# The linear phase of a transformer kernel: its first steps rearranged, the sums of q squares moved beside those of u, and an output projection that waits part by part

## The reference, cut to what matters

```python
q = l2norm(silu(x @ Wq)); k = l2norm(silu(x @ Wk)); v = silu(x @ Wv)
g = sigmoid(x @ Wf - dt_bias); beta = sigmoid(x @ Wb); A = exp(-exp(A_log))
for t in tokens:                      # state: 64x64 for each sequence and head
    o_t = (q_t @ state) * g_t
    state = A * state + beta_t * outer(k_t, v_t)
o = o * rsqrt(mean(o*o) + eps) * norm_w          # over the 64 of a head
out = x + (o * sigmoid(x @ Wg + bg)) @ Wo
```

## Time and profile before

| | us |
|---|---|
| median of 3 runs | 904.65 (904.13 to 906.27) |
| the profiled execution | 908.08 |
| its span, first to last instruction | 906.0 |
| mean granted clock of TensorE | 0.974 |

### The profile page before, as it was taken

The page is one execution under the profiler, slowest core; times in us unless marked ns, Lnnn a source line. Parts: engine busy times, 40 slices in busy tenths (PEclk is TensorE's granted clock), DMA queues, the critical chain, the costliest instruction groups (busy, mean ns, idle before and its releaser), DMA issues.

```text
span 906.0 us, 31429 instructions
## 1 busy us (share of the span) xinstructions
PE 824.8 (91%) x13280; PEld 711.7 (79%) x13280; DVE 554.9 (61%) x1296; ACT 569.4 (63%) x1202; POOL 584.4 (65%) x514
## 2 busy tenths in 40 slices
PE   4858998999797799999999999999999999997877
PEld 3647997899695687888788788888888888885776
DVE  3976566567684356557467467467467467566473
ACT  4746554665565666767767767767767766754544
POOL 4983211320455788977977977977977977986322
PEclk9988999999997899999999999999999999997999
DMA  5001000100100000000000000000000000000011
GB/s 190 26 12 36 25 13 1 31 18 2 25 1 1 1 3 3 4 3 3 3 3 3 4 3 3 4 3 3 4 2 3 3 3 3 3 3 2 13 31 51
DMA packets 19417, 12.38 MB, mean 14 GB/s; under 512 B 7760, under 2 KB 18768, under 8 KB 19024
## 3 DMA queue, kind: packets, MB, share of 16 engines
q1 hardware_dynamic: 19280, 10.39, 4.0%
HBM read 8.29 MB, written 2.10 MB: 11 GB/s over the span
## 4 chain that ended last, share of the span: by engine, by line
PE 50%; DVE 9%; POOL 4%; issue 3%; ACT 2%; DVEq 0%; POOLq 0%; ACTq 0%
PE la_ps L1465 7%; PE la_ps L1467 6%; PE la_ps L1466 6%; DVE la_u_lo L1773 4%; PE la_o_ps L1528 4%; PE la_o_ps L1544 4%; PE la_s_ps L1558 4%; PE la_ps L1575 3%; PE la_ps L1509 3%; DVE la_u L1767 3%; PE la_ps L1609 2%; PE la_ps L1496 2%; PE la_ps L1610 2%; PE la_ps L1611 2%; PE la_ps L1598 1%
## 5 line engine op out<-in xcount | busy, mean ns | idle before, releaser
L2109 POOL TENSOR_TENSOR la_coef<-la_ssk,lt_mhalf 128x32 f32<-128x32 f32 x16 | 87.1, 5442 | 71.2 <-DVE la_ssk L1784 71.2
L1465 PE MATMUL la_ps<-la_x_hi,w_hi 128*128 128x256 f32 x384 | 116.7, 304 | 2.0 <-ACT la_v L1924 1.0
L1467 PE MATMUL la_ps<-la_x_hi,w_lo 128*128 128x256 f32 x384 | 107.6, 280 | 0.1
L1466 PE MATMUL la_ps<-la_x_lo,w_hi 128*128 128x256 f32 x384 | 107.5, 280 | 0.0
L2141 POOL TENSOR_TENSOR la_scale<-la_scale,lt_mhalf 128x32 f32<-128x32 f32 x16 | 99.9, 6241 | 6.7 <-DVE la_scale L1760 6.4
L1807 DVE TENSOR_TENSOR lt_state<-la_s_ps,la_faded 128x512 f32<-128x512 f32 x62 | 42.6, 687 | 70.6 <-PE la_o_ps L1544 57.5
L1465 PEld LDWEIGHTS la_ps<-la_x_hi,w_hi 128*128 128x128 f32 x384 | 72.4, 189 | 14.5 <-issue 6.2
L713 ACT ACTIVATE at_probs<-at_s_ps,at_ntop 128x512 f32<-128x512 f32 (+2 forms) x80 | 49.0, 623 | 46.5 <-DVE at_ntop L655 46.4
L598 PE MATMUL at_o_ps<-V,at_probsT 128*128 128x128 f32 x544 | 74.6, 277 | 3.2 <-DVE at_probsT L507 2.0
L531 POOL CAST at_q_hi<-qk_hi 128x128 fp32r<-128x128 f32 x32 | 9.4, 294 | 104.9 <-PE at_s_ps L572 102.4
L598 PEld LDWEIGHTS at_o_ps<-V,at_probsT 128*128 128x128 f32 x544 | 69.1, 192 | 6.5 <-ACT at_probsT L729 2.3
(11 more groups left out here) (216 smaller groups left out, 2501.3 us busy)
## 6 DMA issues: line engine op xcount, KB each, us to landing
at_w_raw<-in_w SPq DMA_DIRECT2D x20, 128.0 KB, 2.2
X<-in_x SPq DMA_DIRECT2D x8, 256.0 KB, 2.9
out<-X SPq DMA_DIRECT2D x8, 256.0 KB, 2.3
qkv_cos<-in_cos SPq DMA_DIRECT2D x1, 1024.0 KB, 5.0
qkv_sin<-in_sin SPq DMA_DIRECT2D x1, 1024.0 KB, 7.2
lt_w_out<-in_w_out SPq DMA_DIRECT2D x4, 128.0 KB, 2.7
const<-in_const SPq DMA_DIRECT2D x1, 320.5 KB, 3.3
qkv_w<-in_w_qkv SPq DMA_DIRECT2D x1, 320.0 KB, 3.9
```

Source lines behind the costliest of these rows:

```text
L1465: eng.matmul(out, l_hi, r_hi, start=True, stop=False)
L1466: eng.matmul(out, l_hi, r_lo, start=False, stop=False)
L1467: return eng.matmul(out, l_lo, r_hi, start=False, stop=True)
L2109: eng.tensor_tensor(coef[:, :], ssk[:, :], mhalf[:, :], ALU.pow).then_inc(s["coef_step"], 1)
```

## The change

Four things change. `sq` moves in the ring and on PE to right behind `su`, and gets a buffer of its own, `sq_q`, which ACT fills with one instruction behind the last silu of q, a step earlier. `project_out` waits for the low part of u in four parts. In steps -2 to 0 x of tile 1 is turned ahead of `k0` of step -1 (job `x1`), and the copies of it on ACT and `low_x(1)` on POOL move forward with it. The tables' clearing and selectors move from the linear block into the end of the ffn block, `tables.vector` moves the other way, and the first moments and normalized tiles move one and two slots ahead. ACT's list in the linear block begins with a silu of one column.

```diff
@@ ffn_phase, gpsimd slot
+                if next_norm is not None and g.off == GROUPS - 2:
+                    next_norm.first_gpsimd(eng)
                 if tables is not None and g.off == GROUPS - 1:
                     tables.gpsimd_strict(eng)
-                if next_norm is not None and g.off == GROUPS:
-                    next_norm.first_gpsimd(eng)
+                    tables.gpsimd_clear(eng)
+                    tables.gpsimd_selectors(eng)
@@ ffn_phase, vector slot
-                if tables is not None and g.off == GROUPS:
-                    tables.vector(eng)
-                if next_norm is not None and g.off == GROUPS:
-                    next_norm.first_vector(eng)
+                if next_norm is not None and g.off == GROUPS - 1:
+                    next_norm.first_normalized(eng)
...
+                if next_norm is not None and g.off == GROUPS - 2:
+                    eng.wait_ge(x_ready, B)
+                    next_norm.first_moments(eng)
@@ linear_phase
+        sq_q = sb("sq_q", [P, NP, W])
...
-        ring = Ring(("f0 f1 su f2 sT f3 be k0 k1 v0 v1 kT0 kT1 s10 s11 k2 k3 sq sB v2 b0 b1 b2 b3 v3 q0 q1 q2 q3 y g0 g1 yt g2 "
+        ring = Ring(("f0 f1 su sq f2 sT f3 be x1 k0 k1 v0 v1 kT0 kT1 s10 s11 k2 k3 sB v2 b0 b1 b2 b3 v3 q0 q1 q2 q3 y g0 g1 yt g2 "
@@ tensor, betas
+                if n == 0:
+                    eng.wait_ge(tables.loaded, 16 * tables.LOADS)
@@ tensor, project_out
-                eng.wait_ge(s["ulo_ready"], 4 * m)
...
                 for c in range(NP):
+                    if c % 2 == 0:
+                        eng.wait_ge(s["ulo_ready"], 4 * (m - 1) + c // 2 + 1)
@@ tensor, step
                     sum_squares(m, "su")
                 if now:
+                    sum_squares(m, "sq")
                     by_feature(m, "f2")
...
+                if m == -1:
+                    turn_x(1)
...
                 if now:
-                    sum_squares(m, "sq")
                     recall(m, 0, 1)
@@ vector, step
                     add_totals(m)
+                if now:
+                    guard_q(m)
+                if prv:
                     gather_totals(m)
...
                     new_state(m, 0, 0)
-                    guard_q(m)
...
+            tables.vector(eng)
             for m in STEPS[:-1]:
                 step(m)
@@ scalar
-            def square_q(m, half):
-                if half == 0 and m > 0:
-                    written(eng, m, "su")
-                part = slice(half * NP // 2, (half + 1) * NP // 2)
-                eng.activation(sq[:, part, :], qT[:, part, :], ACT.Square).then_inc(s["qsq_ready"], 1)
+            def square_q(n):
+
+                taken(eng, n - 1, "q3")
+                if n > 0:
+                    written(eng, n - 1, "sq")
+                eng.activation(sq_q[:, :, :], qT[:, :, :], ACT.Square).then_inc(s["qsq_ready"], 1)
...
+                if m == -1:
+                    copy_x(1)
...
-                if now:
-                    square_q(m, 0)
...
-                if now:
-                    square_q(m, 1)
...
-                if m == -1:
-                    high_w_out()
+                    if now:
+                        square_q(m + 1)
...
+                if m == -1:
+                    square_q(0)
+                    high_w_out()
...
+            eng.activation(beta[:, 0:1], const[:, C_LEFT:C_LEFT + 1], ACT.Silu)
@@ gpsimd, step
+                if m == -1:
+                    low_x(1)
...
-                if exists(m + 2):
+                if exists(m + 2) and m != -1:
                     low_x(m + 2)
...
-            step(STEPS[0])
-            tables.gpsimd_clear(eng)
-            tables.gpsimd_selectors(eng)
-            for m in STEPS[1:-1]:
+            for m in STEPS[:-1]:
```

More of the change, by code:

```diff
@@ L118, in first_vector, with first_moments, first_normalized @@
             self.moments(eng, Tile(0, k))
+        for k in range(2):
+            self.normalize(eng, Tile(0, k))
+    def first_moments(self, eng):
+        for k in range(2):
+            self.moments(eng, Tile(0, k))
+    def first_normalized(self, eng):
         for k in range(2):
@@ L1382, in has @@
             if job == "xt":
-                return exists(m + 2)
+                return exists(m + 2) and m != -1
+            if job == "x1":
+                return m == -1
             if job in ("su", "sT", "sB", "y", "yt") or job[0] == "b" and job != "be":
@@ L1747, in guard_q @@
             def guard_q(m):
+                if m > 0:
+                    taken(eng, m, "su")
                 bank = written(eng, m, "sq")
```

36 lines of the change are left out of this document (19 added, 17 removed).

## The result

| | before | after |
|---|---|---|
| median of 8 runs each, us | 906.43 (904.13 to 910.98) | 899.44 (898.71 to 902.46) |
| ratio, 95% interval | | 0.9914 [0.9892, 0.9936] |
| the profiled execution | 908.08, span 906.0 | 898.71, span 895.3 |
| mean granted clock | 0.974 | 0.975 |

The change gains 0.86% of the time, 5.8 to 9.8 us by the interval. I had forecast 894.9, a gain of 9.8, with a range from 889.5 to 901.0: the side and the range hold, the point is 4.5 us too low. In its page the chain of work that ended last now lies on PE for 58% of the span and on DVE for 3%.

What follows compares the result with a forecast made beforehand. PE was taken to bound the 13 full steps. Gains of 5.6 (first steps), 0.4 (between the blocks), 1.8 (middle steps) and 2.0 us (last step and drain) sum to 9.8, off a 904.65 median: 894.9 us, range 889.5 to 901.0.

Steps and rivals of the forecast that it cites:

- What bounds the kernel: In the 13 full steps PE bounds, busy 33.58 of 34 us; work elsewhere costs only where PE waits for it.
- First steps: Start of the linear block: the wait ahead of `k0` in step 0 goes, less the squares' cost; 5.6 us gained.
- 6.95: Step 0 up to `attend`: the 4.25 us wait goes and 2.7 us more comes from the clock staying at 2.4 GHz.
- 0.35: First steps: us lost to ACT's 2048-column square ahead of the gates, most of it while PE is in `f0` and `f1`.
- lower end: First steps: the clock falls in step 0 all the same, leaving a gain of 2.9 us.
- Between the blocks: From ffn to linear block: start 1.2 us sooner, less 0.8 for the table load and silu; net 0.4 us gained.
- 279.2 if nothing holds it up: End of POOL's clearing and selectors in the ffn block, 5.3 us of work behind a product ending at 273.9.
- 0.8 us for the table load: Start of the linear block: table load and one-column silu delay ACT's copy of x, 1.5 - 0.7 = 0.8 us.
- Middle steps: The 13 steps: waits for the low part of u shrink, less what the moved squares take back; 1.8 us gained.
- Last step and drain: End of the linear block: state -0.9, projection sooner +1.7, drain wait gone +1.2; 2.0 us gained.
- Slower: Rival: PE waits in each middle step for POOL's keys or DVE's state, outweighing the gain from 0.75 us a step; chance 0.04.
- signs of being wrong: PE waiting for keys or state each step, or gates in `turn_k`; late y copy; low step-0 clock; block at 281 or later.

Runs made afterwards that it cites:

- early x alone: Kernel before with only x of tile 1 turned, copied and its low part taken ahead of `k0` of step -1: 901.78 us, 0.9921.
- squares alone: Kernel before with only `sq` moved on PE, with its buffer, `square_q` and `guard_q` as in the change: 914.67 us, 1.0066.
- blocks undone: Kernel after with the end of the ffn block and POOL's first work as before, no one-column silu: 899.41 us, 0.9889.
- product in the linear block: The early norm kernel with POOL's strict-table product also moved to step -1, behind `low_x(1)`: 893.79 us, 0.9862.
- clearing back: Kernel after with only POOL's clearing and selectors back in the linear block: 895.88 us, 0.9884.
- sum in old place: Waits and early x plus the squares' own buffer and ACT's early square, but PE sums and DVE guards in their old places: 896.80 us, 0.9882.
- product waits: Kernel after with POOL's product waiting until DVE has normalized the two first tiles: 898.30 us, 0.9911.
- early norm: Waits and early x plus earlier roots, moments and normalized tiles; clearing and selectors in the linear block, no one-column silu: 892.80 us, 0.9861.
- waits alone: Kernel before with only the projection's wait for the low part of u split into four parts: 898.76 us, 0.9897.
- waits and early x: Kernel before with the projection waiting by part and x of tile 1 turned ahead of `k0` of step -1: 892.53 us, 0.9848; again 891.34 us, 0.9843.

## Why the prediction was right, and where it was wrong

**What bounds the kernel** held: PE is busy for 33.88 of 34 us in a middle step, and of the waits only those that PE saw paid.

**First steps, 5.6 forecast, 5.4 measured** (from `k0` of step -1 to the first `yt`, 78.9 to 73.5). That they agree is in part luck. The wait and the clock behind it were worth more than 6.95 up to `attend`, which alone came 7.6 us sooner. I had the queries at 308.6 and PE there at the same time; PE waited 0.7 to 0.8, and at the first `yt` 6.1 of the 7.6 were left. For the move of the squares I had 1.35; it cost 2.2 by itself, and 0.7 if the kernel after is held against early x alone (6.1 and 5.4). My "0.35" for ACT's square left out that step 0 has no `y` to cover it: PE waits 1.68 us for the gates. What I didn't see either is that the wait for POOL's keys in step 1, 1.82 us, would go at the same time. And the clock fell at different places, behind the wait for the gates with the squares alone and in step -1 in the kernel after, each worth up to 1.7 us by the estimate; my sum had a low clock only in step 0, as its lower end. So the size of this part isn't shown to better than about 1.5 us.

**Between the blocks, +0.4 forecast, -1.9 measured**, just beyond the -1.0 - 0.8 = -1.8 that was the lowest my bounds allowed: the step that failed. "279.2 if nothing holds it up" was right for POOL (279.1); what was wrong was to take DVE's own end as given, and to look only at what POOL's new work does to POOL's end. DVE ended 0.7 us later in the trace, and 1.2 us later behind its first sum, since its normalizing stood beside POOL's product and clearing. The trace of before had a row with this in it that I did not use: DVE's scaling of the output weights at 271.57 took 2.93 us beside POOL's product and takes 0.75 alone in the linear block of the kernel after. The 0.8 us for the table load was right (`betas` 0.75 later). The drain of 1.4 us that the Trainium skill ("ScalarE: Activation LUTs", "What ACT_TABLE_LOAD costs") adds to each load is not there: the load starts at 281.68, 0.04 before PE's first instruction of the block, and ends at 282.96, and the silu starts at 282.97.

**Middle steps, 1.8 forecast, 4.6 and 6.1 measured** in two traces. The mechanism was right, the term too small: I took 0.25 us of 0.34 a step for what PE sees and 0.1 back for the squares. PE saw all of it, 0.36, in each step, 4.7 us over 13. The squares take 0.11 to 0.13 a step back where the projection waits by part (0.2 where it doesn't). That makes 3.0 to 3.3 us. The 1.4 and 2.9 us that were measured above it stay without a cause; two traces of one kernel differ by up to 1.8 here, and of the kernel before there is one.

**Last step and drain, 2.0 forecast, 2.3 and 1.3 measured.** +1.7 and +1.2 came as summed. The state cost 1.5 to 1.7, not 0.9: beside DVE's later start, `sq` had left the place where it lay in that wait. With the sum back in its place the wait is 2.94 us, against 4.36 in blocks undone.

**The rivals.** "Slower" had its mechanism: the state is late once `sq` no longer stands in front of it. But it costs 0.2 us a step in the kernel with the squares alone and stays under 0.75. PE waited for POOL's keys 0.5 us once in the middle steps. Of my signs of being wrong two came: a wait for ACT's gates in `turn_k`, in step 0, and the block starting at 281.72.

**The total.** In the traces the gain is 10.7 us of span: 0.4 ahead of the first sum into X, -1.9, 5.4, 4.6 and 2.3, each rounded. The forecast 9.8 comes near it since the 2.3 us missed between the blocks were made up by 2.8 in the middle steps; that is luck, not a right sum. The medians differ by 7.0. Of the 4.5 us by which 894.9 is low, 1.8 is the base (904.65 from 3 runs, 906.43 from 8). The rest is within the spread of single executions, 904.1 to 911.0 for the kernel before: the profiled execution of before, at 908.08, was one of its slower ones and that of after, at 898.71, one of the fastest. So the 3.4 us that I had put down to profiling are this spread too.

## What to carry to other kernels

Where a consumer reads a tile in parts, wait for the parts: two lines were worth 9 us here. Before an independent job is moved off its place on the bounding engine, ask what it was standing in front of; a job that fills a wait is free only there, and a cover that every middle step has may be missing in the first. Before a difference of 1 to 3 us between two traces is given to an edit, lay the granted clock of the same stretch beside it. When work moves on POOL, lay it beside DVE's timeline for that stretch, not only into POOL's sum.

## What the runs showed of the hardware

- A DVE operation of 0.3 us, the second normalizing of tile 1, lasted 4.8 us beside POOL's product and clearing (the row at 269.90 holds it and one of 1.3 us).
- The granted clock fell a second time in step -1, in both traces of the kernel after and in that with the product in the linear block, and in none of the other kernels. In all fourteen traces PE had just stood still for 1.0 us for ACT's silu of v. Four microseconds from the scores on, in the kernel after and in that with the clearing back (busy time of PE, PEld, DVE, ACT, POOL, then the clock and DMA):

```profile
298.00:302.00 4.00, 3.91 (x75) 3.83 (x76) 1.66 (x3) 3.92 (x5) 4.00 (x1) 0.57 0.02 4
```

```profile
295.20:299.20 4.00, 4.00 (x95) 3.23 (x95) 1.80 (x3) 4.00 (x6) 4.00 (x1) 1.00 0.02 4
```

The clock is near the lower of its two levels (1.2 GHz) in the one and at the upper (2.4 GHz) in the other; the scores took 1.99 us and 1.16. From `betas` of step -1 to those of step 0 it is 21.2 us and 19.5. What decides it these runs don't show: PE's work in the stretch is the same.
- It fell in the same way later in the first steps in six traces: behind the wait of 1.68 us for ACT's gates in step 0 in blocks undone, q squares alone, sum in old place and product waits, but in neither trace of the kernel after and not with the clearing back, where PE waits there for as long; and behind the wait of 1.8 us for POOL's keys in step 1 in the two kernels with early norm, but not in before, the waits alone, early x alone and both traces of waits and early x. Four microseconds from the end of the wait for the gates, in blocks undone and in the kernel after:

```profile
325.06:329.06 4.00, 3.98 (x144) 3.76 (x144) 0.00 (x0) 2.28 (x6) 3.84 (x4) 0.64 0.02 4
```

```profile
326.36:330.36 4.00, 3.88 (x152) 3.61 (x152) 0.79 (x2) 2.29 (x6) 3.84 (x4) 1.00 0.01 4
```

From `attend` to the first `yt` the kernels with early x take 51.9 to 52.2 us where the clock fell in that stretch and 49.9 to 51.3 where it didn't. So of two traces that differ there by 1 or 2 us, the edit needn't be the cause.
- In the last step the clock falls in every kernel, in or behind PE's wait for DVE's state (in waits by part alone only behind the next one, for the low part of u), and when it comes back differs between two executions of one kernel. The end of that step in the two traces of waits and early x:

```profile
820.00:830.40 10.40, 9.10 (x49) 8.73 (x50) 6.17 (x10) 4.83 (x10) 1.65 (x1) 0.60 0.01 2
```

```profile
817.70:826.40 8.70, 7.26 (x48) 6.89 (x49) 6.18 (x10) 4.92 (x9) 1.66 (x1) 0.80 0.01 2
```

At 0.60 this stretch, from `spread_scales` to `yt`, is 1.7 us longer than at 0.80; from the end of the wait for the state (817.00 and 814.14) it is 13.4 and 12.3 us, since in the second trace the clock fell sooner (its mean over the 4 us from there is 0.52, and 0.63 in the first). That is 1.1 of the 1.6 us between 34.3 and 32.8. So 1 or 2 us in the last step of a single trace can't be told from nothing.
